# Row statistics of x taken once ahead of the scans, in a layer of a selective scan and a mixture of experts

## The chip, the cores and the metric

The program runs on one core of one Trainium2 chip. The metric is the device time of one execution in microseconds, and what is compared is the median over runs. Each core has five engines that work at the same time and wait for one another by semaphores: PE (TensorE, matmuls and transposes), DVE (VectorE), ACT (ScalarE), POOL (GpSimd) and SP (SyncE, which here only starts transfers). Transfers run on 16 DMA engines.

## What is computed

The input x has 4096 rows (tokens) of 256 numbers. Two sublayers follow one another, each of the form `x = x + layernorm(f(layernorm(x)))`. The first `f` is a selective scan, the second a router with the two best of 8 experts for each token plus a shared expert. Cut to what matters:

```python
xn = x * jax.lax.rsqrt(jnp.mean(x * x, -1, keepdims=True) + EPS) * norm_w   # x is layernorm(x) here
xg = xn @ in_proj_w
x_inner, gate = jnp.split(xg, 2, axis=-1)
x_inner = x_inner * jax.nn.silu(gate)
xc = causal_conv(x_inner, conv_w)                 # 4 taps, per channel
dt = jax.nn.softplus(xc @ dt_w + dt_b)
Bm, Cm = xc @ B_w, xc @ C_w
h = exp(dt * A) * h + dt * Bm * xc                # over time, for 512 channels x 16 states
y = sum_over_states(h * Cm) + D_skip * xc
out = y @ out_proj_w
...
x = x + _layernorm(selective_scan(_layernorm(x)))
x = x + _layernorm(experts(_layernorm(x)) + shared_expert(_layernorm(x)))
```

The layernorm of x and the rms norm after it need only the mean and the variance of each row of x, so the kernel takes both at once: one scale and one shift for each row.

## The kernel before

**Chunks and loops.** The 4096 rows are cut into 8 chunks of 512 (`NCH = 8`, `CH = 512`), a chunk into 4 row tiles of 128 rows (`J = 4`). A chunk is scanned in 64 slots (`SLOTS`, k = 0 to 63): one slot for each of 16 states times 4 groups of 128 channels. The outer loop runs from -2 to 9. In loop n the scans of chunk n stand slot by slot in each engine's program, and between them stands the work of other chunks: the projections of chunk n+1 (`*_proj`), the output, the norms and the routing of chunk n-1 (`*_post`), and the first norm of chunk n+2 (`*_lead`). In loops -2 and -1 there are no scans yet; this stretch is called the run-in here. After loop 9 the experts follow (71 row tiles).

**A slot.** ACT makes the decay `exp(dt*A)` (L735) into one of two banks. POOL multiplies the input (L1018) into one of four buffers. DVE scans over 512 steps (L861). PE turns the result of a state (L591), and DVE multiplies three quarters of it by C and adds it up (L878, L875), while ACT takes the fourth (L754). DVE runs on an input as soon as both the decay and the input are there.

**What sets the order.** Each engine runs its program strictly in the order in which it is written. Tables of slot numbers (`LEAD`, `PROJ` and `POST` for PE; `ACT_AT`, `DVE_AT`, `POOL_AT`) say behind which scan each piece of the other work stands. PE's results of this other work go in turn through three banks (`A`, `NQ = 3`); a bank is used again when its reader has emptied it (`room`). The list of turns comes from the same tables.

**The first norm of a chunk.** SP loads the chunk's x into `xp` (L348, slot 24). DVE takes `bn_stats` of 4 row tiles (L767, slot 48) and `bn_aggr` (L774, slot 49). POOL makes the variance term (L923, slot 50), ACT a first root by Ln and Exp (L615, L617, slot 51), POOL one Newton step of six small instructions (`newton`, L131 to L140, slot 53), then ACT normalizes the four tiles into `xn` (L624, slot 55), PE turns them (L439, slot 61) and ACT copies them into `xnT` (L628). For chunks 0 and 1 this stands in loops -2 and -1, for chunks 2 to 7 in loops 0 to 5, between scans.

**The run-in.** SP starts eight loads of weights and constants, then x of chunk 0, then the later weights (`late_weights`), then x of chunk 1. DVE scales `in_proj_w` by `norm_w` (L1153) and builds the four taps of the convolution as diagonal matrices (L1160), and all engines but SP wait for the end of this (`s_cst` at 5) before their loops. ACT first makes `-exp(A_log)` (L1105, L1107). Then chunk 0 passes through first norm, gates (PE L452), inner projection (PE L462, DVE L783), convolution (PE L472, ACT L647), B and C (`bT`: PE L480, ACT L652), dt (PE L491, ACT L663 to L670, POOL L939 and L943).

**Routing, at the end of a loop.** PE ranks the tokens of each expert (`rank`, L544 and L546, slot 60). DVE adds the result to the running base (`place`, L832, and `base`, L836) and multiplies the shared expert's three parts (`sgs`, L847), whose silu is done by ACT (L712, between two loads of its table).

Of the kernel before, what the change touches and what calls it, by code (L numbers as in the profile page):

```python
# [142 lines left out]
def program(nc, sem, sb, top, x_rows, out_rows, norm_w, in_proj_w, conv_w, dt_w, dt_b, A_log, B_w, C_w, D_skip,  # L143
# [619 lines left out]
    def dve_lead(e, k, c):  # L763
# [5 lines left out]
        if k == DVE_AT["stats_x"] + 1:  # L769
            e.wait_ge(s_cx, 2 * c + 1)  # L770
            if c:
                e.wait_ge(s_p0n, c)
# [722 lines left out]
```

## Time and profile before

| | us |
|---|---|
| median of 3 runs | 1716.26 |
| lowest and highest of them | 1711.7, 1716.83 |
| the profiled execution | 1713.8 |
| its span in the trace | 1712.0 |
| first scan starts | 80.49 |
| last scan starts | 1055.9 |

The profile is that of one execution. Its times count from the start of the span; the execution's own time is 1.8 us longer than the span. An engine counts as busy while an instruction of its runs. A matmul on 512 columns stands as two records in the trace.

### The profile page before, as it was taken

Reading aid. Unit: us, or ns where it says so; the run is one execution under the profiler, and the core shown is the slowest. Engines: PE = TensorE matmul, PEld = TensorE weight load, DVE = VectorE, ACT = ScalarE, POOL = GpSimd, SP = SyncE. Lnnn points to the kernel's source line nnn. Section 1 sums busy time; section 2 is a strip of 40 time slices with the busy share of each in tenths; the row PEclk is TensorE's granted clock in tenths of the full one; section 3 lists DMA queues with packets and bytes.
Section 4 is the critical chain, followed back from the end, with each engine's and each line's share of the span. In section 5 each row is a group of like instructions: output and inputs, shape, how many; then the busy total and the mean of one; then the engine's idle time right before and its main releaser. Section 6 shows DMA issues by size and latency. Waiting matters only on the chain.

```text
span 1712.0 us, 23925 instructions
## 1 busy us (share of the span) xinstructions
PE 1500.3 (88%) x6642; PEld 996.5 (58%) x6642; DVE 1353.0 (79%) x2425; ACT 1000.6 (58%) x1977; POOL 1043.6 (61%) x1233
## 2 busy tenths in 40 slices
PE   5888699899999998998998668699999999999990
PEld 2355455555655655745655555467677777777760
DVE  2199999899999899999899998256576676676665
ACT  3456667667668668659668564334454454454454
POOL 0478869979979879879889886312222322322224
PEclk9889899999999999999999968799999999999995
DMA  3011111311211221221211752523322222222216
GB/s 114 32 50 38 50 43 51 108 46 51 81 62 38 82 56 38 85 59 36 83 51 44 232 166 73 169 51 75 91 38 35 37 37 36 36 38 36 37 30 202
DMA packets 84398, 116.23 MB, mean 68 GB/s; under 512 B 11120, under 2 KB 58576, under 8 KB 84272
## 3 DMA queue, kind: packets, MB, share of 16 engines
q1 hardware_dynamic: 63344, 82.94, 16.0%
q0 software_dynamic: 16704, 27.57, 8.3%
q10 hardware_dynamic: 4224, 4.19, 0.7%
q8 instruction: 60, 0.98, 0.2%
q14 instruction: 66, 0.54, 0.1%
HBM read 81.05 MB, written 33.10 MB: 67 GB/s over the span
## 4 chain that ended last, share of the span: by engine, by line
PE 33%; POOL 6%; DVE 5%; issue 5%; ACT 2%; DMA 1%; SPq 0%; POOLq 0%; DVEq 0%; ACTq 0%
PE A L1244 10%; PE bA L1213 10%; PE bH L1213 10%; POOL arena L1018 4%; DVE arena L861 2%; DVE arena_t L878 1%; PE A L1235 1%; POOL expert_in_scratch L1006 1%; PE A L521 1%; DMA arena_t<-expert_in_scratch 0%; PE bH L591 0%; DMA sum_scratch<-arena_t 0%; DVE arena L878 0%; PE A L554 0%; DVE hT L1267 0%
## 5 line engine op out<-in xcount | busy, mean ns | idle before, releaser
L1018 POOL TENSOR_TENSOR arena<-arena 128x512 f32<-128x512 f32 x512 | 643.9, 1274 | 101.7 <-DVE arena L861 99.3
L735 ACT ACTIVATE bA<-arena,a_neg 128x512 f32<-128x512 f32 x512 | 352.1, 691 | 258.8 <-DVE arena L861 242.2
L591 PEld LDWEIGHTS bH<-ident,arena 128*128 128x128 f32 x2048 | 247.3, 146 | 303.0 <-DVE arena L861 139.3
L591 PE MATMUL bH<-ident,arena 128*128 128x128 f32 x2048 | 326.3, 287 | 93.9 <-DVE arena L861 72.9
L861 DVE TENSOR_TENSOR_SCAN arena<-bA,arena 128x512 f32<-128x512 f32 x256 | 305.7, 1210 | 63.6 <-ACT bA L735 48.8
L861 DVE TENSOR_TENSOR_SCAN arena<-bA,hl,arena 128x512 f32<-128x512 f32 x256 | 321.5, 1271 | 3.8 <-ACT bA L735 2.0
L1277 ACT COPY hT<-arena_t 32x160 f32<-32x160 f32 x568 | 182.5, 321 | 77.3 <-DVE arena_t L1261 71.6
L1267 DVE STREAM_TRANSPOSE hT<-arena_t 32x192 f32<-32x192 f32 x568 | 205.9, 363 | 6.6
L1371 POOL DMA_INDIRECT sum_scratch<-arena_t x71 | 113.5, 1598 | 148.6 <-issue 119.6
L1244 PE MATMUL A<-arena,hT 128*128 x852 | 197.5, 382 | 2.1 <-DVE hT L1267 2.1
L1365 POOL DMA_DIRECT2D arena_t<-expert_in_scratch x71 | 40.6, 573 | 257.5 <-issue 257.5
L1431 DVE TENSOR_TENSOR arena_t<-arena_t,bH 128x352 f32<-128x352 f32 x142 | 67.6, 518 | 151.1 <-PE bH L1213 151.1
L1213 PE MATMUL bA<-arena,arena_t 128*128 x568 | 181.5, 463 | 1.4 <-ACT arena_t L1413 1.4
L1213 PE MATMUL bH<-arena,arena_t 128*128 x568 | 179.6, 459 | 0.0
L1244 PEld LDWEIGHTS A<-arena,hT 128*128 128x128 f32 x852 | 157.6, 192 | 21.5 <-issue 2.5
L1213 PEld LDWEIGHTS bH<-arena,arena_t 128*128 128x128 f32 x568 | 107.9, 190 | 60.1
L1213 PEld LDWEIGHTS bA<-arena,arena_t 128*128 128x128 f32 x568 | 108.6, 192 | 51.3 <-issue 3.3
L878 DVE SCALAR_TENSOR_TENSOR arena<-bH,bc,arena 128x512 f32<-128x512 f32 x180 | 131.3, 729 | 5.7 <-PE bH L591 5.2
L878 DVE SCALAR_TENSOR_TENSOR arena_t<-bH,bc,arena_t 128x512 f32<-128x512 f32 x180 | 131.2, 729 | 3.8 <-PE bH L591 3.2
L472 PE MATMUL A<-arena 128*128 128x512 f32 x256 | 123.0, 593 | 0.0
L1413 ACT COPY arena_t<-A 128x256 f32<-128x256 f32 x71 | 26.5, 373 | 128.4 <-PE A L1235 128.4
L1407 ACT ACTIVATE arena_t<-bA 128x352 f32<-128x352 f32 x142 | 58.1, 461 | 72.6 <-PE bA L1213 72.6
(191 smaller groups left out, 2042.0 us busy)
## 6 DMA issues: line engine op xcount, KB each, us to landing
arena<-b_scratch SPq DMA_DIRECT2D x128, 256.0 KB, 3.2
arena_t<-expert_in_scratch POOLq DMA_DIRECT2D x71, 132.0 KB, 2.4
arena<-in_L_ffn_Wg_dram SPq DMA_DIRECT2D x8, 704.0 KB
arena<-in_L_ffn_Wu_dram SPq DMA_DIRECT2D x8, 704.0 KB
arena<-in_L_ffn_Wd_dram SPq DMA_DIRECT2D x8, 640.0 KB
arena<-in_L_attn_x_dram SPq DMA_DIRECT2D x8, 512.0 KB, 5.1
arena_x<-in_L_attn_x_dram SPq DMA_DIRECT2D x8, 512.0 KB, 5.1
x_scratch<-arena_x SPq DMA_DIRECT2D x8, 512.0 KB, 3.2
```

What stands on the lines that cost most here:

```text
L472: i = e.matmul(at(b, c)[:], w_tap[:, d, q, :], xin[:, d, q:q + CH], start=(q == 0), stop=(q == TAPS - 1))
L591: i = e.transpose(bH[g % NH][:, q * P:(q + 1) * P], hh[:, (n - 1) % 2, q, d * P:(d + 1) * P], ident[:])
L735: e.activation(bA[g % NA][:], dt[c % 2][:, d, :], ACT.Exp, scale=a_neg[:, d, n:n + 1]).then_inc(s_a, 1)
L861: e.tensor_tensor_scan(hh[:, n % 2, d, :], bA[g % NA][:], bb[:, k % NB, :], hl[:, n, d:d + 1] if c % 2 else 0.0, ALU.mult, ALU.add).then_i ...
L878: e.scalar_tensor_tensor(out=yy[:, d, :], in0=bH[g % NH][:], scalar=cm, in1=yy[:, d, :], op0=ALU.mult, op1=ALU.add).then_inc(s_y, 1)
L1018: e.tensor_tensor(bb[:, k % NB, :], u[c % 2][:, d, :], br[:, n % NR, :], ALU.mult).then_inc(s_bb, 1)
L1213: i = e.matmul(banks[f][:, 0:FH], xtT[:, t % 2, k, :], arena[:, bass.ds(ex * EW + (o + k * FI + f * FH), FH)], start=(k == 0), stop=(k == ...
L1244: i = e.matmul(bD[t % 2][:, 0:DM], hT[:, t % 2, q, :], arena[:, bass.ds(ex * EW + (2 * KD * FI + q * DM), DM)], start=(q == 0), stop=(q == ...
L1267: i = e.transpose(out, in_)
L1277: i = e.copy(out, in_)
L1371: e.indirect_dma_start(out=sh_d, out_offset=bass.IndirectOffsetOnAxis(ap=xt[:].bitcast(U32)[:, (t - 1) % NX, TOK:TOK + 1], axis=0), in_=yt ...
L1431: i = e.tensor_tensor(hm[:, t % 2, f * FH:(f + 1) * FH], sgm[:, t % 2, f * FH:(f + 1) * FH], bU[f][:, 0:FH], ALU.mult)
```

## The change

The mean and variance of x are no longer taken chunk by chunk between scans. They are taken in two groups: chunk 0 alone, first of all on DVE, and chunks 1 to 7 together (28 row tiles) in loop -1, behind the inner projection of chunk 0. For this SP loads x of chunks 1 to 7 a second time, 3.67 MB, into buffers that are still unused (`hh`, `bb`, `xf`), and `hs` holds the raw statistics. `mv`, `va`, `r0`, `tn` and `nmr` now hold all 32 row tiles. POOL's variance term and Newton step and ACT's two roots are done twice in all, in place of eight times. x of chunk 0 is the first transfer, ahead of the weights. The scaling of `in_proj_w` and the taps come behind the statistics of chunk 0 on DVE, `-exp(A_log)` behind the first norm on ACT, and the waits for `s_cst` are moved to where their data are used. The tables of slots are changed in some places.

```diff
-PROJ = {"gate0": 2, "gate1": 1, "gate2": 9, "gate3": 9, "inner0": 12, "inner1": 18, "inner2": 20, "inner3": 18, "cv0": 21, "cv1": 23, "cv2": 26,
-        "cv3": 30, "bT": 33, "dt0": 36, "bc": 37, "dt1": 42, "dt2": 45, "dt3": 50}
+PROJ = {"gate0": 2, "gate1": 1, "gate2": 9, "gate3": 8, "inner0": 12, "inner1": 17, "inner2": 20, "inner3": 18, "cv0": 21, "cv1": 23, "cv2": 26,
+        "cv3": 30, "bT": 33, "dt0": 36, "bc": 40, "dt1": 40, "dt2": 45, "dt3": 50}
...
-DVE_AT = {"stats_x": 48, "inner": (15, 19, 24, 21), "y": (9, 7, 5, 7), "stats_out": (19, 22), "stats_xf": 34, "logit": 52, "max": 54, "index": 54,
-          "place": 59, "base": 59, "position": 62, "sgs": (60, 63, SLOTS)}
+DVE_AT = {"inner": (15, 19, 24, 21), "y": (9, 7, 5, 7), "stats_out": (19, 22), "stats_xf": 35, "logit": 52, "max": 54, "index": 54, "place": 59,
+          "base": 60, "position": 63, "sgs": (SLOTS, 59, SLOTS + 1)}
...
+    STAGE = [(1, 4, row_tiles(hh[:].rearrange("p a b c -> p (a b c)"))), (5, 2, row_tiles(bb[:].rearrange("p a b -> p (a b)"))), (7, 1, xf[:, :, 0:DM])]
+    GROUP = [slice(0, J), slice(J, NCH * J)]
...
+    def sp_stage(e):
+        for c, n, to in STAGE:
+            e.dma_start(to, x_rows[c * CH:(c + n) * CH, :].rearrange("(r p) d -> p r d", p=P)).then_inc(s_xs, 16)
...
+    def dve_stats_x(e, g):
+        if g == 0:
+            e.wait_ge(s_x, 16)
+            tiles = [xp[:, j, :] for j in range(J)]
+        else:
+            e.wait_ge(s_xs, 16 * len(STAGE))
+            tiles = [to[:, j, :] for c, n, to in STAGE for j in range(n * J)]
+        for j, t in enumerate(tiles):
+            i = e.bn_stats(st[:, g * J + j, :], t)
+        i.then_inc(s_cx, 1)
+        e.wait_ge(s_cx, 2 * g + 1)
+        for j in range(len(tiles)):
+            i = e.bn_aggr(mv[:, g * J + j, :], st[:, g * J + j, :])
+        i.then_inc(s_cx, 1)
...
     def sync_scan(e):
+        e.dma_start(xp[:], rows_of(x_rows, 0)).then_inc(s_x, 16)
         e.dma_start(w_in[:], in_proj_w.rearrange("(k p) n -> p k n", p=P)).then_inc(s_w, 16)
...
             if loop == -1:
                 late_weights(e)
+                sp_stage(e)
...
+                if (loop, k) == (-1, 30):
+                    pool_var_x(e, 1)
+                if (loop, k) == (-1, 41):
+                    pool_norm_x(e, 1)
...
+                if (loop, k) == (-1, 38):
+                    act_root_x(e, 1)
...
+                if (loop, k) == (-1, 26):
+                    dve_stats_x(e, 1)
```

In the shared expert's work `su0` and `su1` change places (slots 58 and 62 become 62 and 58), `su2` goes from 62 to 63, ACT's copy of `bT` from 36 to 38, POOL's `halo` from 7 to 10.

Three places show how the instructions move. The first is the start of DVE's program; `arena` holds among others x, the weights and, in the new order, the staged rows; `ident` and `w_cv` make the taps. First the kernel before, then the changed one:

```order
1 L1149 MEMSET hT 64x2x128
2 L1153 TENSOR_SCALAR arena<-arena,w_nm 128x1024 x2
3 L1155 CAST iota_e<-iota_i 128x8
4 L1156 CAST base<-capi 128x8
5 L1160 TENSOR_SCALAR arena<-ident,w_cv 128x128 x16
6 L767 BN_STATS st<-arena 128x6 x4
7 L774 BN_AGGR mv<-st 128x2 x4
```

```order
1 L1178 MEMSET hT 64x2x128
2 L786 BN_STATS hs<-arena 128x6 x4
3 L790 BN_AGGR mv<-hs 128x2 x4
4 L1183 TENSOR_SCALAR arena<-arena,w_nm 128x1024 x2
5 L1185 CAST iota_e<-iota_i 128x8
6 L1186 CAST base<-capi 128x8
7 L1190 TENSOR_SCALAR arena<-ident,w_cv 128x128 x16
8 L799 TENSOR_TENSOR arena<-arena,A 128x512 x4
9 L786 BN_STATS hs<-arena 128x6 x24
10 L786 BN_STATS hs<-arena_x 128x6 x4
11 L790 BN_AGGR mv<-hs 128x2 x28
12 L877 SCALAR_TENSOR_TENSOR arena<-bA,arena 128x512 x6
```

The statistics of chunk 0 have moved ahead of the scaling and the taps, and all the others stand between the inner products (L799) and the first scans (L877, printed as SCALAR_TENSOR_TENSOR).

The second place is DVE at slots 59 to 61 of loop 1, behind the last scan that the ranks wait for; `pos` and `base` belong to the routing, `arena_x<-arena_x,A` is a part of `sgs`. Before, then changed:

```order
219 L832 TENSOR_TENSOR pos<-A,base 128x32
220 L836 TENSOR_TENSOR base<-base,A 128x8
221 L861 SCALAR_TENSOR_TENSOR arena<-bA,hl,arena 128x512
222 L847 TENSOR_TENSOR arena_x<-arena_x,A 128x512
223 L861 SCALAR_TENSOR_TENSOR arena<-bA,hl,arena 128x512
```

```order
215 L848 TENSOR_TENSOR pos<-A,base 128x32
216 L863 TENSOR_TENSOR arena_x<-arena_x,A 128x512
217 L877 SCALAR_TENSOR_TENSOR arena<-bA,hl,arena 128x512
218 L852 TENSOR_TENSOR base<-base,A 128x8
219 L877 SCALAR_TENSOR_TENSOR arena<-bA,hl,arena 128x512
```

One product of the shared expert now stands ahead of scan 60, and `base` behind it.

The third place is SP's queue behind the late weights, ahead of the first rows of B (`b_scratch`). Before, then changed:

```order
16 L428 DMA arena_x<-in_L_ffn_Sd_dram 96x256
17 L348 DMA arena<-in_L_attn_x_dram 128x4x256
18 L353 DMA b_scratch<-arena 16x512
19 L371 DMA arena<-b_scratch 128x512 x10
```

```order
16 L439 DMA arena_x<-in_L_ffn_Sd_dram 96x256
17 L359 DMA arena<-in_L_attn_x_dram 128x16x256
18 L359 DMA arena<-in_L_attn_x_dram 128x8x256
19 L359 DMA arena_x<-in_L_attn_x_dram 128x4x256
20 L355 DMA arena<-in_L_attn_x_dram 128x4x256
21 L364 DMA b_scratch<-arena 16x512
```

The three staging loads stand between the weights and the load of chunk 1's x.

## Rows read from the trace of the kernel before

**Rows 1.** The page's first line.

```profile
span 1712.0 us, 23925 instructions
```

**Rows 2.** Windows: length; busy us of PE, PEld, DVE, ACT, POOL; clock; DMA; GB/s.

```profile
197.00:320.00 123.00, 110.73 (x550) 68.40 (x549) 120.11 (x165) 87.49 (x143) 100.38 (x113) 1.00 0.19 58
320.00:441.00 121.00, 109.59 (x543) 68.88 (x542) 112.15 (x158) 86.12 (x140) 106.89 (x128) 1.00 0.20 58
```

**Rows 3.** Groups, DVE, 80 to 1057 us: busy us, mean ns | idle before.

```profile
L767 DVE BATCH_NORM_STATS2 st<-arena 128x6 f32<-128x256 f32 x24 | 8.3, 409 | 0.0
```

**Rows 4.** Timeline (start us, us) of DVE, slots 48 and 49 of loop 1.

```profile
286.88 1.39 DVE L767 BATCH_NORM_STATS2 st<-arena 128x6 f32<-128x256 f32 x4
288.18 1.28 DVE L861 TENSOR_TENSOR_SCAN arena<-bA,hl,arena 128x512 f32<-128x512 f32 x1
...
290.00 0.38 DVE L774 BATCH_NORM_AGGREGATE mv<-st 128x2 f32<-128x6 f32 x4
290.29 1.26 DVE L861 TENSOR_TENSOR_SCAN arena<-bA,hl,arena 128x512 f32<-128x512 f32 x1
```

**Rows 5.** Timeline of DVE, slots 59 to 61 of loop 1; [idle before <-releaser].

```profile
309.58 0.19 DVE L832 TENSOR_TENSOR pos<-A,base 128x32 f32<-128x32 f32 x1 [1.12 <-PE A L546]
309.81 0.16 DVE L836 TENSOR_TENSOR base<-base,A 128x8 f32<-128x8 f32 x1
310.55 1.28 DVE L861 TENSOR_TENSOR_SCAN arena<-bA,hl,arena 128x512 f32<-128x512 f32 x1 [0.57 <-ACT bA L735]
311.75 0.66 DVE L847 TENSOR_TENSOR arena_x<-arena_x,A 128x512 f32<-128x512 f32 x1
312.32 1.28 DVE L861 TENSOR_TENSOR_SCAN arena<-bA,hl,arena 128x512 f32<-128x512 f32 x1
```

**Rows 6.** ACT in order of time at the same place.

```profile
307.02 1.48 ACT L712 ACTIVATE arena_x<-arena_x 128x1536 f32<-128x1536 f32 x1
308.52 1.28 ACT L714 ACT_TABLE_LOAD   x1
309.82 1.30 ACT L735 ACTIVATE bA<-arena,a_neg 128x512 f32<-128x512 f32 x2
```

**Rows 7.** The run-in in order of time, all engines.

```profile
8.28 1.42 DVE L1153 TENSOR_SCALAR arena<-arena,w_nm 128x1024 f32<-128x1024 f32 x2 [6.96 <-DMA dskip<-in_L_attn_D_skip_dram]
...
13.01 1.41 DVE L767 BATCH_NORM_STATS2 st<-arena 128x6 f32<-128x256 f32 x4
...
22.25 9.92 PE L452 MATMUL A<-arena 128*128 128x512 f32 x16 [0.77 <-ACT arena L628]
...
40.04 0.69 DVE L783 TENSOR_TENSOR arena<-arena,A 128x512 f32<-128x512 f32 x1 [1.89 <-PE A L462]
...
57.29 0.57 ACT L652 COPY arena<-A 32x512 f32<-32x512 f32 x1 [3.89 <-PE A L480]
```

**Rows 8.** The end of the run-in in order of time.

```profile
73.75 0.63 ACT L670 ACTIVATE arena<-arena 128x512 f32<-128x512 f32 x1
...
75.14 2.07 ACT L624 ACTIVATE arena<-arena,nmr,r 128x256 f32<-128x256 f32 x4 [0.77 <-POOL nmr L140]
...
80.49 5.68 DVE L861 TENSOR_TENSOR_SCAN arena<-bA,arena 128x512 f32<-128x512 f32 x5 [38.03 <-ACT bA L735]
```

**Rows 9.** Line L348's loads of x; then windows, last column GB/s.

```profile
DMA to landing us min/median/max: 3.8/5.1/5.2
...
8.00:18.00 10.00, 0.00 (x0) 0.00 (x0) 6.48 (x28) 2.87 (x7) 1.42 (x8) 1.00 0.98 316
18.00:20.00 2.00, 0.45 (x2) 0.48 (x3) 0.00 (x0) 1.40 (x3) 0.00 (x0) 1.00 0.01 2
```

**Rows 10.** Groups, PE: gate matmuls of chunk 0 before and after 27.9 us.

```profile
L452 PE MATMUL A<-arena 128*128 128x512 f32 x7 | 6.1, 1043 | 0.8 <-ACT arena L628 0.8
...
L452 PE MATMUL A<-arena 128*128 128x512 f32 x9 | 4.2, 616 | 0.0
```

**Rows 11.** ACT's first norm during the scans, 100 to 1050 us.

```profile
L624 ACT ACTIVATE arena<-arena,nmr,r 128x256 f32<-128x256 f32 x24 | 12.5, 593 | 1.0 <-POOL nmr L140 1.0
```

More of the change, by code:

```diff
@@ L57 @@
-POOL_AT = {"var_x": 50, "norm_x": 53, "halo": 7, "skip": 36, "dt": (43, 49, 51, 58), "var_out": 23, "norm_out": 28, "add": (31, 31, 31, 31),
-           "var_xf": 38, "norm_xf": 40, "diff": 55, "token": 47, "chosen": 56, "picked": 61, "gates": SLOTS, "scatter": SLOTS + 1}
+        "su0": 62, "su1": 58, "su2": 63, "sd0": SLOTS + 3, "sd1": SLOTS + 7}
+ACT_AT = {"gate": (4, 3, 11, 10), "silu": 14, "conv": (26, 25, 28, 33), "bT": 38, "bc": 42, "dt": (40, 45, 49, 53), "norm_x": (55, 55, 55, 55),
+          "xnT": (60, 61), "out": (16, 19), "root_out": 27, "norm_out": (30, 31, 31, 31), "root_xf": 39, "xf": (41, 44, 44, 45), "xfT": (50, 46),
+          "e2": 60, "sg": (58, 56, 55), "sg_silu": 58, "sd": (SLOTS + 5, SLOTS + 8), "sum": 3}
@@ L60 @@
+DVE_AT = {"inner": (15, 19, 24, 21), "y": (9, 7, 5, 7), "stats_out": (19, 22), "stats_xf": 35, "logit": 52, "max": 54, "index": 54, "place": 59,
+          "base": 60, "position": 63, "sgs": (SLOTS, 59, SLOTS + 1)}
+POOL_AT = {"halo": 10, "skip": 36, "dt": (43, 49, 51, 58), "var_out": 23, "norm_out": 28, "add": (31, 31, 31, 31), "var_xf": 38, "norm_xf": 39,
+           "diff": 55, "token": 47, "chosen": 56, "picked": 61, "gates": SLOTS, "scatter": SLOTS + 1}
 LATE = {("sd0", NCH - 2): SLOTS + 24, ("sd1", NCH - 2): SLOTS + 26, ("sd", NCH - 2): (SLOTS + 26, SLOTS + 28),
@@ L759, in act_summed @@
             e.copy(xc[(c - 1) % 2][:, :, 0:P], bY[:].rearrange("p (d t) -> p d t", d=ND)).then_inc(s_y0, 1)
-    def dve_lead(e, k, c):
-        if k == DVE_AT["stats_x"]:
-            e.wait_ge(s_x, 16 * (c + 1))
-            for j in range(J):
-                i = e.bn_stats(st[:, j, :], xp[:, j, :])
-            i.then_inc(s_cx, 1)
[L769 to L772, printed above, removed]
-            for j in range(J):
-                i = e.bn_aggr(mv[:, j, :], st[:, j, :])
-            i.then_inc(s_cx, 1)
+    def dve_stats_x(e, g):
[12 more added lines that the diff above has]
+        i.then_inc(s_cx, 1)
     def dve_proj(e, k, c):
@@ L1130, in pe_scan @@
         e.wait_ge(s_id, 3)
-        e.wait_ge(s_cst, 5)
         for loop in range(-2, NCH + 2):
+            if loop == -1:
+                e.wait_ge(s_cst, 2)
             for k in range(SLOTS):
+                if (loop, k) == (-1, min(PROJ[name] for name in CONVS)):
+                    e.wait_ge(s_cst, 5)
                 if 0 <= loop < NCH or loop == NCH and k < ND:
```

78 lines of the change are left out of this document (39 added, 39 removed).

## The prediction

> **What bounds the kernel now.** I read the page first for the span, 1712.0 us [rows 1], and then cut it into stages: a run-in to the first scan at 80.49 us [rows 8], the scans, and the experts. The change touches the first two; the experts begin when the last chunk is routed and should only shift. So the question is what ends last in the run-in, and in a chunk of scans.
>
> For the scans I asked for busy time in stretches of one chunk. In an odd chunk DVE is busy 120.1 of 123 us, in an even one 112.2 of 121 [rows 2]. No other engine comes near in the odd one (PE 110.7, POOL 100.4, ACT 87.5); in the even one POOL follows with 106.9. DVE is thus the bound in odd chunks, with 2.9 us idle, and nearly so in even ones, with 8.9 us idle in which it waits in turn for ACT, POOL and PE. An instruction that leaves DVE's program between scans should give back its whole step, so long as the others can follow.
>
> For the run-in I read the instructions in order of time [rows 7, 8]. Chunk 0 goes through it as one chain: statistics at 13.01, gate matmuls at 22.25, inner product at 40.04, copy of `bT` at 57.29, last dt step of ACT at 73.75, first norm of chunk 1 at 75.14, first scan at 80.49. The statistics start at 13.01 without a wait [rows 7]: DVE had been working since 8.28 on the scaling and the taps, and had waited for the constants before that. DVE is idle from the inner products to the first scan, 38 us [rows 8].
>
> **The change, part by part.**
>
> *Run-in, start.* x of chunk 0 becomes the first transfer, issued where `in_proj_w` was, at about 0.9 us (an estimate: SP's first issue follows the start of all engines, the MEMSETs of which stand near 1 us). The loads of x took 3.8 to 5.2 us from issue to landing [rows 9]; the shortest is that of chunk 1, with nothing else under way. With 3.8 the statistics start at 4.7, with 5.2 at 6.1. I take 3.8, since nothing is ahead of it. From statistics to gate matmuls it took 22.25 - 13.01 = 9.24 us [rows 7], a chain over DVE, POOL, ACT and PE that is not changed. The gates then start at 14.0, which is 8.3 us earlier (6.9 with the late landing). They also need the scaled `in_proj_w`. Its data and all constants had landed by 8.28 [rows 7]; 0.5 MB more ahead of them costs 1.7 us at 316 GB/s [rows 9], so about 10.0, and the two scalings take 1.4: ready at 11.4, hidden by 2.6 us. The taps follow and end near 15, needed only by the convolution. ACT's `-exp(A_log)` moves into its wait for the gates. All of this shifts the chain by 8.3 us.
>
> Whether the whole chain shifts depends on the clock of PE. The gate matmuls up to 27.9 us took 1043 ns in the mean, those behind it 616 [rows 10]: first the lower of PE's two levels (1.2 GHz), then the upper (2.4). PE's first work stands just ahead of these. If the rise goes with that work, it moves too, and the gates keep their 8.3 us. If it came at a fixed time of the program, all gates up to 27.9 would be slow: 27.9 - 14.0 = 13.9 us at half speed in place of 27.9 - 22.25 = 5.65, a loss of (13.9 - 5.65)/2 = 4.1 us. The trace of before can't tell the two apart. The Trainium skill, page "TensorE: Matmul & The Clock Gate", Part 1, says that the default is the throttled clock and that activity of the array releases it; by that the first holds and the second, 4.1 us dearer, doesn't.
>
> *Run-in, end.* ACT finished dt at 74.38 (73.75 + 0.63) and waited 0.77 us for POOL's Newton step before it normalized chunk 1 [rows 8]. The step is now done long before, so 0.8 us more is gained, and the path stays norm, turn, copy, decay, scan. POOL's inputs, ready before ACT's first decay (the scan at 80.49 waited for ACT), come earlier by the same 8.3 us and by the Newton step that stood before them, so they don't hold the scan. The first scan starts at 80.5 - 8.3 - 0.8 = 71.4. **Term A: -9.1 us** (-7.7 with the late landing).
>
> *Staging.* 3.67 MB are added on SP's queue behind the late weights and ahead of chunk 1's x and of B's rows. The transfers up to then ended at 18 us, after 316 GB/s over ten microseconds, and the next two microseconds moved almost nothing [rows 9]; the bytes to that point are the same in the changed kernel. The staging ends at 18 + 3670/316 = 29.6 us. DVE comes to it behind the last inner product, at 40.04 + 0.69 - 8.3 = 32.4. Four `bn_stats` step DVE on by 288.18 - 286.88 = 1.30 us, four `bn_aggr` by 0.29 [rows 4]; 28 of each are 7 x 1.59 = 11.1 us, to 43.5. POOL's and ACT's small steps behind it are under 1.5 us. Queued behind the root on ACT is the copy of `bT`, due at 57.29 - 8.3 = 49.0 [rows 7], and behind that PE's next dt products, which need its bank. The slack is 49.0 - 1.5 - 43.5 = 4 us, and 2.8 us more for the transfer, which may land late without cost until DVE is there. The cover is DVE's idle stretch of 38 us; if it were gone the 11.1 us would be paid. Cost taken: nothing.
>
> *Scans.* `stats_x` leaves DVE in loops 0 to 5, for six chunks: 24 `bn_stats`, 8.3 us busy [rows 3], and 24 `bn_aggr`. Busy times overlap their neighbours; the step is 1.30 + 0.29 = 1.59 us [rows 4]. **Term B: 6 x 1.59 = -9.5 us.** With them go seven small instructions on POOL and two on ACT for each chunk. POOL is the nearest rival in even chunks, and what it loses is of the same size: its Newton steps take some 0.2 to 0.3 us each. So POOL doesn't keep DVE from the gain. ACT waited 1.0 us in all for the Newton step [rows 11]; I count half of it on the path. **Term C: -0.5 us.**
>
> *Slots 59 to 61.* There, once in each of loops 1 to 7, DVE waits 1.12 us for PE's ranks, does `place` and `base`, and waits 0.57 us for ACT's decay, which comes behind silu and a table load [rows 5, 6]. The changed order puts one `sgs` product into this second wait: it took a step of 312.32 - 311.75 = 0.57 us behind scan 60, and `base` (0.1 us of step) goes out of the wait. The first wait stays. Saved 0.57 - 0.1 = 0.47, seven times. **Term D: -3.3 us.** The product waits for ACT's silu, which ends at 308.5 [rows 6], and DVE gets there at 309.8 [rows 5]: 1.3 us of room. The other moved slots (gate3, inner1, dt1, bc, su2, halo) shift PE and POOL work by one to three slots, where PE has 10 us of idle time in a chunk; nothing for them, bounded by 0.3 us a chunk to either side, 2 us in all.
>
> *Discount.* ACT runs without a gap from silu to the decay of slot 60 [rows 6], so that DVE, 1.6 us ahead, may find it late in some chunks. Of term B I expect 1 us to be lost so.
>
> **Sum.** -9.1 - 9.5 - 0.5 - 3.3 + 1.0 = -21.4 us against the profiled execution's 1713.8 us, which gives 1692.4. The median of the runs shown is 2.5 us above it, 1716.3, and runs agree within 5 us; the same sum on the median gives **1695 us**. A change under 0.3%, 5 us, can't be told from none.
>
> **The rivals.**
>
> 1. *ACT and PE take back what DVE gives.* For: ACT has no gap ahead of slot 60 [rows 6], PE is busy 90% of a chunk [rows 2], and even chunks have waits for three engines. Against: both are only in places full, and ACT loses work too. If two thirds of B and all of C and D are lost: -9.1 - 3.2 = -12.3, **1704 us**.
> 2. *The clock rises at its own time.* The run-in gains 9.1 - 4.1 = 5.0 only: -17.3, **1699 us**. For it: nothing in the trace speaks against. The page's rule above is against it.
> 3. *The staging is late.* Chunk 1's x alone took 3.8 us for 0.5 MB [rows 9], 138 GB/s with its start. At that rate the staging takes 26.6 us, to 44.6, the statistics end at 55.7, and `bT` is copied at 57.2 in place of 49.0; PE has 1.7 us of other products first. Loss 6.5 us: -14.9, **1701 us**.
> 4. *Slower: the product at slot 59 holds DVE.* It needs ACT's silu and PE's `su1`. If ACT comes there later than DVE by d, each of 7 chunks pays d, and the end is slower when 7 d is over 21.4 us, d over 3.1 us. ACT would have to fall back by 1.3 + 3.1 = 4.4 us against DVE. At d = 4.1 it gives 1716.3 + 7 = **1723 us**. Against: ACT's work is less than before.
> 5. *Little changes*: both halves fail in part, within 5 us of **1716 us**.
>
> **How the numbers follow.** The forecast, 1691 to 1699 (landing at 5.2 us costs 1.4, the slots 2 to either side, the runs 2), has 0.68. Rival 1 has 0.14, rival 2 0.07, rival 3 0.05, rival 4 0.03, rival 5 0.03. All of the forecast and of 1 to 3 is over 0.3% faster: 0.94; within 0.3%: 0.03; slower: 0.03. The range takes in rivals 1 to 3 and 8 us below the forecast, for gains in waits that I have counted at nothing in the even chunks (8.9 us of DVE's idle time each): 1687 to 1706.
>
> **What would show it.** Term A: first scan at 71 to 73 us, gate matmuls at 14, the slow ones ending near 19.6. Staging: landed by 30, 28 `bn_stats` from 32.4, `bT` copied without a wait for POOL. Terms B to D: last scan 21 us earlier than 1055.9, so the scans 12 us shorter than 975, DVE's busy time 10 us less from first to last scan, its idle time in a chunk no longer than before; the wait for ACT at slot 60 gone, that for the ranks still 1.1 us. The prediction is wrong if DVE's idle time rises by more than 1 us in a chunk, if a wait for `s_sil` of the shared expert appears on DVE at slot 59, or if the experts' stage changes its length by more than 2 us.

## The result and the profile after

The changed kernel took 1688.57 us in the median of 4 runs (1687.43 to 1688.84), beside 1714.45 (1711.7 to 1716.83) for the kernel before: a ratio of 0.9848, interval 0.983 to 0.9867. The forecast was 1695, range 1687 to 1706. A second set on another chip gave 0.9859 (0.9844 to 0.9874). The profiled execution took 1688.78 us, 1.7 us longer than its span. The two spans differ by 24.9 us:

| stretch | before | after | difference |
|---|---|---|---|
| to the first scan | 80.5 | 70.7 | -9.8 |
| first to last scan | 975.4 | 961.5 | -13.9 |
| behind the last scan's start | 656.1 | 654.9 | -1.2 |

The page's first line and two windows, loops 1 and 2, with the columns of [rows 2]:

```profile
span 1687.1 us, 23869 instructions
...
181.50:303.10 121.60, 110.28 (x541) 68.06 (x540) 117.41 (x155) 86.77 (x140) 98.51 (x102) 0.99 0.20 59
303.10:426.60 123.50, 114.20 (x566) 71.61 (x565) 115.43 (x158) 87.70 (x142) 108.84 (x129) 1.00 0.19 61
```

They are cut at the scans that begin a loop, a little off the round cuts of [rows 2]. For the sum I took one window from first to last scan in each kernel, of before and of after:

```profile
80.50:1055.90 975.40, 860.31 (x4212) 547.97 (x4210) 928.22 (x1246) 666.87 (x1069) 830.82 (x941) 0.96 0.23 68
```

```profile
70.70:1032.20 961.50, 859.03 (x4211) 547.34 (x4210) 919.54 (x1196) 663.85 (x1057) 824.02 (x899) 0.96 0.22 69
```

DVE's busy time fell by 8.7 us, its idle time from 975.4 - 928.2 = 47.2 to 42.0, by 5.2. Only the first part is the statistics. This division, busy and idle time of DVE between first and last scan, is the measure used below.

**The run-in**, rows of all engines in order of time, to be read beside [rows 7, 8]:

```profile
4.96 1.41 DVE L786 BATCH_NORM_STATS2 hs<-arena 128x6 f32<-128x256 f32 x4 [3.65 <-DMA arena<-in_L_attn_x_dram]
...
9.81 1.42 DVE L1183 TENSOR_SCALAR arena<-arena,w_nm 128x1024 f32<-128x1024 f32 x2 [3.02 <-DMA dskip<-in_L_attn_D_skip_dram]
...
14.20 1.19 PE L463 MATMUL A<-arena 128*128 128x512 f32 x1 [0.77 <-ACT arena L643]
...
31.10 0.69 DVE L799 TENSOR_TENSOR arena<-arena,A 128x512 f32<-128x512 f32 x1 [1.86 <-PE A L473]
31.70 7.93 DVE L786 BATCH_NORM_STATS2 hs<-arena 128x6 f32<-128x256 f32 x24
39.55 1.39 DVE L786 BATCH_NORM_STATS2 hs<-arena_x 128x6 f32<-128x256 f32 x4
40.98 1.95 DVE L790 BATCH_NORM_AGGREGATE mv<-hs 128x2 f32<-128x6 f32 x28
...
44.36 0.23 ACT L626 ACTIVATE r<-va 128x28 f32<-128x28 f32 x1
...
48.35 0.57 ACT L667 COPY arena<-A 32x512 f32<-32x512 f32 x1 [3.50 <-PE A L491]
...
70.68 1.22 DVE L877 TENSOR_TENSOR_SCAN arena<-bA,arena 128x512 f32<-128x512 f32 x1 [27.75 <-ACT bA L750]
```

Every link stands within 0.8 us of where the sum put it: statistics 4.96 (4.7 forecast), `in_proj_w` scaled by 11.2 (11.4), gates 14.20 (14.0), group of 28 from 31.70 (32.4), `bT` copied at 48.35 (49.0), first scan 70.68 (71.4). The 28 `bn_stats` start without a wait, and the copy of `bT` waited for PE alone. The gate matmuls of chunk 0, in two windows that part at 18.9 us:

```profile
L463 PE MATMUL A<-arena 128*128 128x512 f32 x7 | 5.2, 905 | 0.8 <-ACT arena L643 0.8
...
L463 PE MATMUL A<-arena 128*128 128x512 f32 x11 | 4.9, 592 | 0.0
```

In the kernel before PE was slow until 27.9 us [rows 10]; now it is fast by 18.9. In the three kernels with the old run-in (the kernel before, and stats_only and new_tables of the experiments) the first gate matmul of under 600 ns starts at 26.7 to 28.2 us, in the eleven with the new one at 17.3 to 20.1. The rise of the clock went with PE's work and not with the time. That is what the Trainium skill says in "TensorE: Matmul & The Clock Gate", Part 1; by that page the gates keep their whole gain, and the trace agrees (14.20 to 22.25 is 8.05 us).

**In a loop.** DVE and ACT in loop 1, at the norm of the next chunk and at slots 59 to 61 [rows 4 to 6]:

```profile
288.53 1.28 DVE L877 TENSOR_TENSOR_SCAN arena<-bA,hl,arena 128x512 f32<-128x512 f32 x1 [0.56 <-ACT bA L750]
...
295.25 0.19 DVE L848 TENSOR_TENSOR pos<-A,base 128x32 f32<-128x32 f32 x1 [1.12 <-PE A L557]
295.35 0.68 DVE L863 TENSOR_TENSOR arena_x<-arena_x,A 128x512 f32<-128x512 f32 x1
296.21 1.28 DVE L877 TENSOR_TENSOR_SCAN arena<-bA,hl,arena 128x512 f32<-128x512 f32 x1 [0.18 <-ACT bA L750]
```

```profile
285.84 2.08 ACT L639 ACTIVATE arena<-arena,nmr,r 128x256 f32<-128x256 f32 x4
287.82 0.68 ACT L750 ACTIVATE bA<-arena,a_neg 128x512 f32<-128x512 f32 x1
...
295.49 1.30 ACT L750 ACTIVATE bA<-arena,a_neg 128x512 f32<-128x512 f32 x2
```

The product stands where the wait for ACT was, and 0.18 of 0.57 us is left; the wait for the ranks is still 1.12. New is a wait of 0.56 us at 288.53: DVE, no longer held by the statistics, comes to this scan while ACT is still in its four normalizations. In even loops the like happens with POOL. DVE in loop 4 before (the first two rows) and after:

```profile
659.20 1.22 DVE L861 TENSOR_TENSOR_SCAN arena<-bA,arena 128x512 f32<-128x512 f32 x1 [0.72 <-POOL hl L1030]
676.40 2.34 DVE L861 TENSOR_TENSOR_SCAN arena<-bA,arena 128x512 f32<-128x512 f32 x2 [1.40 <-ACT bA L735]
```

```profile
640.71 2.34 DVE L877 TENSOR_TENSOR_SCAN arena<-bA,arena 128x512 f32<-128x512 f32 x2 [0.32 <-POOL hl L1046]
648.53 1.22 DVE L877 TENSOR_TENSOR_SCAN arena<-bA,arena 128x512 f32<-128x512 f32 x1 [1.29 <-POOL hl L1046]
```

The wait of 1.40 us for ACT behind the normalizations is gone, and one of 1.29 for POOL's copy of the carried state (`hl`, made at every fourth slot) stands a few slots ahead of its place. POOL's five instructions ahead of that copy (642.08 to 648.19) follow one another without a gap, so the copy can't come earlier in this order. In loop 4 before, the time that DVE spent on statistics had covered this. The trace of before showed this already, in loop 6, which has no statistics and no norm of a next chunk:

```profile
916.67 1.22 DVE L861 TENSOR_TENSOR_SCAN arena<-bA,arena 128x512 f32<-128x512 f32 x1 [1.28 <-POOL hl L1030]
```

### The profile page after: what moved, and what is told of

It is laid out like the page before. It is cut to its first block, busy times and chain, and to the rows that moved or that the text cites. A ratio compares the mean times of both kernels' runs of the same rounds, so it can differ in the third digit from the quotient of the medians.

```text
span 1687.1 us, 23869 instructions
## 1 busy us (share of the span) xinstructions
PE 1494.5 (89%) x6642; PEld 993.3 (59%) x6642; DVE 1353.8 (80%) x2425; ACT 996.3 (59%) x1964; POOL 1038.9 (62%) x1191
## 4 chain that ended last, share of the span: by engine, by line
PE 33%; POOL 6%; DVE 5%; issue 5%; ACT 2%; DMA 2%; SPq 0%; POOLq 0%; DVEq 0%; ACTq 0%
PE A L1274 10%; PE bA L1243 10%; PE bH L1243 10%; POOL arena L1034 3%; DVE arena L877 2%; DVE arena_t L894 1%; PE A L1265 1%; DMA sum_scratch<-arena_t 1%; POOL expert_in_scratch L1022 1%; DMA arena_t<-expert_in_scratch 0%; PE bH L602 0%; PE A L532 0%; DVE arena L894 0%; ACT bA L750 0%; POOL rr L138 0%
## 5 line engine op out<-in xcount | busy, mean ns | idle before, releaser
L602 PEld LDWEIGHTS bH<-ident,arena 128*128 128x128 f32 x2048 | 250.9, 147 | 300.4 <-DVE arena L877 129.8
L877 DVE TENSOR_TENSOR_SCAN arena<-bA,arena 128x512 f32<-128x512 f32 x256 | 305.8, 1211 | 50.0 <-ACT bA L750 33.2
L877 DVE TENSOR_TENSOR_SCAN arena<-bA,hl,arena 128x512 f32<-128x512 f32 x256 | 321.6, 1271 | 2.5 <-ACT bA L750 2.1
L1274 PEld LDWEIGHTS A<-arena,hT 128*128 128x128 f32 x852 | 157.5, 191 | 21.4 <-issue 2.5
L769 ACT ACTIVATE hs<-bH,bc 128x512 f32<-128x512 f32 x128 | 87.5, 683 | 33.8 <-PE bH L602 32.5
```

The costliest lines, as they stand in the source:

```text
L602: i = e.transpose(bH[g % NH][:, q * P:(q + 1) * P], hh[:, (n - 1) % 2, q, d * P:(d + 1) * P], ident[:])
L769: e.activation(hs[:, q % 2, :], bH[(c * SLOTS + k) % NH][:], ACT.Identity, scale=bc[cs % 2][:, 0, NS + q % NS:NS + q % NS + 1]).then_inc(s ...
L877: e.tensor_tensor_scan(hh[:, n % 2, d, :], bA[g % NA][:], bb[:, k % NB, :], hl[:, n, d:d + 1] if c % 2 else 0.0, ALU.mult, ALU.add).then_i ...
L1274: i = e.matmul(bD[t % 2][:, 0:DM], hT[:, t % 2, q, :], arena[:, bass.ds(ex * EW + (2 * KD * FI + q * DM), DM)], start=(q == 0), stop=(q == ...
```

## The experiments

Four kernels ran on each of three chips, beside the kernel before, which took 1709.36, 1708.64 and 1709.6 us there. A saving against the kernel before is worked out from the ratio; from the medians it comes out up to 1 us different. Two kernels of one chip are compared by their medians. A ratio is known to some 0.0015, 2.5 us, so a difference of two ratios to some 0.002, 3.6 us. Two theories stand in the expectations. Theory 1: each part pays what the sum gave it. Theory 2: the total is made up otherwise, by the clock of PE in the first loop or by waits that other engines' work sets; its numbers were drawn anew after the first four runs, as the texts say.

| kernel | run-in | statistics once | new tables | ratio | interval | scans | busy DVE | idle DVE |
|---|---|---|---|---|---|---|---|---|
| before | | | | 1 | | 975.4 | 928.2 | 47.2 |
| runin_only | x | | | 0.9947 | 0.9933 to 0.9962 | 980.3 | 928.5 | 51.8 |
| stats_only | | x | | 0.9970 | 0.9961 to 0.9980 | 973.4 | 920.3 | 53.1 |
| new_tables | | | x | 0.9963 | 0.9948 to 0.9977 | 969.0 | 928.4 | 40.6 |
| old_tables | x | x | | 0.9919 | 0.9905 to 0.9934 | 970.6 | 920.1 | 50.5 |
| changed kernel | x | x | x | 0.9848 | 0.9830 to 0.9867 | 961.5 | 919.5 | 42.0 |

The last three columns are of one profiled execution each. That of runin_only took 1705.17 us where its median is 1700.78, so some 4 us of its idle time are not typical. The length of single loops in what follows is from these traces too, from first scan to first scan.

**runin_only**: the new order of the run-in and nothing else.

```diff
+        e.dma_start(xp[:], rows_of(x_rows, 0)).then_inc(s_x, 16)      # first of all on SP
...
+        dve_lead(e, DVE_AT["stats_x"], 0)                             # DVE, ahead of the scaling
+        dve_lead(e, DVE_AT["stats_x"] + 1, 0)
```

> The kernel before with the new order of the run-in alone: x of chunk 0 first, its statistics ahead of the scaling and the taps, the waits moved; the statistics of the other chunks stay between scans and the tables of slots are the old ones. Theory 1 (the sum of the prediction): 8.3 us less than the kernel before, first scan at 72.2 us, scans of unchanged length. Theory 2 (what the changed kernel's trace suggests: the first loop of scans also gains, because the granted clock of PE was back at 1.00 at 83 us there and only near 120 us before): about 10.5 us less, the first loop of scans some 2.3 us shorter than 116.0.

It took 1700.78 us beside 1709.36, 9 us less, with the first scan at 72.4. The run-in pays its term and the first loop keeps its length (116.1 us, before 116.0). Theory 2's guess that a better clock in loop 0 comes with the earlier start has no support here: over the first 35 us of scans the granted clock is 0.77, before 0.78.

**stats_only**: statistics once, but x of chunk 0 loaded and taken in the old order, and the old tables; the diff is against the changed kernel.

```diff
-        e.dma_start(xp[:], rows_of(x_rows, 0)).then_inc(s_x, 16)
         e.dma_start(w_in[:], in_proj_w.rearrange("(k p) n -> p k n", p=P)).then_inc(s_w, 16)
...
+        e.dma_start(xp[:], rows_of(x_rows, 0)).then_inc(s_x, 16)
```

> The changed kernel with the old order of the run-in (x of chunk 0 behind the weights, its statistics behind the taps) and the old tables of slots: the statistics of chunks 1 to 7 in one group are what is left of the change. Theory 1: 9.5 + 0.5 + 0.8 = 10.8 us less than the kernel before, 1.6 us in each of loops 0 to 5. Theory 2 (odd loops give DVE's time back as waits for ACT and PE, even loops gain on POOL): about 8 to 9 us less, with at most 1 us in loops 1, 3 and 5 and 2 us or more in loops 0, 2 and 4.

1703.98 us, 5.1 less than before; both theories expected more (10.8, and 8 to 9). The first scan is 1.4 us earlier (79.04), and from first to last scan DVE is busy 7.9 us less and idle 5.9 us more. Most of the step that DVE saves is taken back by waits. Against the kernel before, loops 0, 2 and 4 are 1.9, 0.3 and 2.4 us shorter, loops 1 and 3 are 1.5 and 0.5 longer and loop 5 is 0.4 shorter. So the pattern is roughly that of Theory 2, and the sizes are smaller.

**old_tables**: the changed kernel with the old tables. One of their lines:

```diff
-DVE_AT = {"inner": (15, 19, 24, 21), ... "place": 59, "base": 60, "position": 63, "sgs": (SLOTS, 59, SLOTS + 1)}
+DVE_AT = {"inner": (15, 19, 24, 21), ... "place": 59, "base": 59, "position": 62, "sgs": (60, 63, SLOTS)}
```

> The changed kernel with the old tables of slots. Theory 1: 3.3 us slower than the changed kernel, DVE waits 0.5 us for ACT at slot 60 again. Theory 2 (the tables gave at slot 60 and took it back as waits for PE near slot 14 of odd loops, 1.3 us in loop 1): within 1.5 us of the changed kernel.

1695.55 us, 0.9919: the sum of the two savings before it, 14 us. It is slower than the changed kernel by 0.0060 to 0.0071, 10 to 12 us, so both theories failed (3.3, and within 1.5). Where the statistics' step goes in an odd loop is seen in loop 3, DVE's rows that have a wait, and then PE at the end of the loop:

```profile
539.00 1.28 DVE L877 TENSOR_TENSOR_SCAN arena<-bA,hl,arena 128x512 f32<-128x512 f32 x1 [0.56 <-ACT bA L750]
...
545.71 0.19 DVE L848 TENSOR_TENSOR pos<-A,base 128x32 f32<-128x32 f32 x1 [1.12 <-PE A L557]
...
546.61 1.28 DVE L877 TENSOR_TENSOR_SCAN arena<-bA,hl,arena 128x512 f32<-128x512 f32 x1 [0.51 <-ACT bA L750]
...
553.94 0.75 DVE L894 SCALAR_TENSOR_TENSOR arena_t<-bH,bc,arena_t 128x512 f32<-128x512 f32 x1 [0.42 <-PE bH L602]
554.87 0.69 DVE L863 TENSOR_TENSOR arena_x<-arena_x,A 128x512 f32<-128x512 f32 x1 [0.18 <-PE A L574]
```

```profile
546.00 0.60 PE L450 MATMUL A<-ident,arena 128*128 128x128 f32 x4
548.62 1.09 PE L450 MATMUL A<-ident,arena 128*128 128x128 f32 x4 [2.01 <-DVE arena_x L863]
...
551.20 2.26 PE L574 MATMUL A<-arena_x 128*128 128x512 f32 x4
553.30 0.60 PE L602 MATMUL bH<-ident,arena 128*128 128x128 f32 x4
```

```profile
546.00:556.00 10.00, 7.99 (x35) 5.43 (x34) 8.89 (x13) 5.51 (x10) 7.26 (x11) 0.83 0.27 82
```

Of 1.59 us, 0.56 go to ACT's normalizations, 0.6 to PE, whose turn of a state stands behind four records of the shared expert's products (L574), and 0.21 to another wait for PE. The 0.6 us go with PE's clock. PE waited 2.01 us for a bank that DVE's product `sgs` empties; behind that wait the same four matmuls take 1.09 us in place of 0.60, and the granted clock of the stretch is 0.83 (last row). In loop 5 of stats_only the clock stays at 1.00 there, and the 0.6 us are missing.

This wait of PE, 1.9 to 2.2 us, stands in each of loops 1 to 5 of all six kernels with the old tables, the kernel before among them, and in none of the eight with the new ones, where this product stands at slot 59 and not at 60. Beside 15 of these 30 waits the granted clock fell, and in those loops DVE then waited 0.2 to 2.2 us for PE at the loop's end; beside the other 15 it didn't. In loops 1 to 5 of the eight kernels with the new tables the clock fell at a loop's end once in 40. So a part of what the tables give, 2.5 us of DVE's idle time in old_tables and 0.7 in the kernel before, is a clock that stays up, as far as these traces show it; no run isolates it.

Loops 1, 3 and 5 took 123.5, 123.7 and 124.0 us, where the kernel before took 122.1, 123.3 and 123.5. The even loops 2 and 4 took 125.3 and 123.8, before 125.6 and 126.2.

**new_tables**: the kernel before with the new slots for the work that stays.

```diff
-DVE_AT = {"stats_x": 48, ... "place": 59, "base": 59, "position": 62, "sgs": (60, 63, SLOTS)}
+DVE_AT = {"stats_x": 48, ... "place": 59, "base": 60, "position": 63, "sgs": (SLOTS, 59, SLOTS + 1)}
```

> The kernel before with the new tables of slots alone; statistics and run-in as before. Theory 1: 3.3 us less than the kernel before. Theory 2: within 1.5 us of it, with DVE's wait for PE longer near slot 14 of odd loops.

1703.32 us, 6.3 less (3.9 to 8.9), with DVE's busy time unchanged and 6.6 us less of idle time: about twice term D, and far from Theory 2's 1.5. The waits for ACT at slot 60 fell from 3.3 us over loops 1 to 7 to 1.3, less than forecast. The rest came from elsewhere: 1.6 us of it lie in loop 0, most of them in waits for PE, and at the end of loop 4 the wait for PE at the low clock (0.7 us) is gone. At the start of loops 2, 4 and 6 DVE waited for POOL's `hl` 2.97, 2.75 and 2.78 us before and 2.37, 2.17 and 2.17 here, later in them 0.7 and now 0.3 us, and in the odd loops three waits of 0.6 us for POOL's input are gone, while PE's turn is waited for 0.35 us longer there (0.9 in loop 1). One row of it, DVE in loop 2:

```profile
334.98 2.34 DVE L861 TENSOR_TENSOR_SCAN arena<-bA,arena 128x512 f32<-128x512 f32 x2 [2.37 <-POOL hl L1030]
```

With the new table two products `sgs` (0.6 us each) stand behind the first scan of a loop, in place of one. DVE does the second one where it would wait for POOL anyway. The sizes fit, but that this entry alone does it was argued and not tried.

**after_again, early_hl, spread_norm, both**: the changed kernel once more, and two edits to it and their union.

> The changed kernel once more, beside which the next three stand. Theory 1 (each part pays what the sum gave it) and Theory 2 (the run-in pays its 9 us, the statistics half of their step, the new tables twice or more of theirs) both expect what was measured: 1686 to 1690 us, 1.3 to 1.7% under the kernel before.

0.9859 (0.9844 to 0.9874), 1684.55 us beside 1708.64.

```diff
-        if c % 2 == 0 and k % ND == ND - 1 and k > ND:      # pool_last, the copy of hl
+        if c % 2 == 0 and k % ND == 0 and k >= ND:          # three slots earlier
```

> The changed kernel with POOL's copy of the carried state moved by one step: at the first of four products of a pair of scans in place of the last of the four. In the changed kernel DVE waits for that copy 2.5 to 5.0 us in each even loop, 17 us in all. If these waits have taken the place of what the removed statistics gave (Theory 2), most of them go away: 8 to 14 us faster than the changed kernel, 1675 to 1680, with no POOL wait above 0.3 us in a loop. If POOL's throughput is the bound there (rival), the copy only pushes POOL's next products later, the waits for POOL come back at another instruction, and the time stays within 3 us of the changed kernel.

1677.27 us, 0.9818 (0.9804 to 0.9831): 7.3 us faster than the changed kernel, just under the 8 to 14 expected and well over the rival's 3, and DVE idle 34.0 us. POOL and DVE at the start of loop 2, first in the changed kernel:

```profile
316.20 1.00 POOL L1022 DMA_INDIRECT expert_in_scratch<-arena_x,posl  x1 [0.17 <-issue]
317.50 0.97 POOL L1022 DMA_INDIRECT expert_in_scratch<-arena_x,posl  x1 [0.30 <-issue]
318.50 2.50 POOL L1034 TENSOR_TENSOR arena<-arena 128x512 f32<-128x512 f32 x2
320.94 0.18 POOL L1046 COPY hl<-arena 128x4 f32<-128x4 f32 x1
321.25 2.34 DVE L877 TENSOR_TENSOR_SCAN arena<-bA,arena 128x512 f32<-128x512 f32 x2 [2.39 <-POOL hl L1046]
```

```profile
318.58 2.45 DVE L877 TENSOR_TENSOR_SCAN arena<-bA,arena 128x512 f32<-128x512 f32 x2
...
324.77 1.22 DVE L877 TENSOR_TENSOR_SCAN arena<-bA,arena 128x512 f32<-128x512 f32 x1 [0.80 <-POOL arena L1034]
```

The copy stood behind POOL's scattering of rows for the experts. Moved ahead of it, all waits for `hl` are gone from loops 2, 4 and 6 (5.0 us in loop 2), and about 3 us of it stay gained in each; 0.8 us come back at the next input of POOL and 1.3 us as waits for PE. In loop 0, 2.6 us of waits for `hl` are gone too, but the loop is no shorter (110.9 us beside 110.8 and 110.1). So POOL was partly late by order and partly by amount, between the theory and its rival.

```diff
-  ... "norm_x": (55, 55, 55, 55), ...
+  ... "norm_x": (54, 55, 56, 57), ...
```

> The changed kernel with ACT's four normalizations of the next chunk at slots 54, 55, 56 and 57, in place of four behind each other at slot 55. They are a burst of about 2 us, in which ACT's decays stand behind them. If the burst is what makes DVE wait for ACT (0.56 us in each odd loop, about 1 us in each even one), the waits at that place vanish and it is 2 to 5 us faster than the changed kernel. The rival: the normalization feeds the transposes and the gates of the next chunk, and spreading it makes DVE's wait for PE longer by as much; then it is within 2 us.

1692.15 us, 0.9899 (0.9884 to 0.9914): slower than the changed kernel by 7.6 us. Both expectations failed (2 to 5 us faster, and within 2). ACT and DVE in loop 3:

```profile
537.30 0.59 ACT L639 ACTIVATE arena<-arena,nmr,r 128x256 f32<-128x256 f32 x1
...
539.00 1.28 ACT L727 ACT_TABLE_LOAD   x1
...
543.09 1.30 ACT L750 ACTIVATE bA<-arena,a_neg 128x512 f32<-128x512 f32 x2
```

```profile
537.40 1.28 DVE L877 TENSOR_TENSOR_SCAN arena<-bA,hl,arena 128x512 f32<-128x512 f32 x1 [0.51 <-ACT bA L750]
...
543.82 1.28 DVE L877 TENSOR_TENSOR_SCAN arena<-bA,hl,arena 128x512 f32<-128x512 f32 x1 [0.75 <-ACT bA L750]
```

From the normalizations to the decay of slot 60 ACT has next to no gap, so the wait for the burst stays as 0.51 us, one slot on, and with less room before silu the wait at slot 60, gone from this loop in the changed kernel, is back with 0.75. In each of loops 1 to 5 the idle time is 0.6 to 0.9 us longer than in after_again. Spreading the burst moved its wait and added one.

> The changed kernel with both edits, the earlier copy of the carried state and the spread normalization. If the two kinds of wait are independent, the gains add: 10 to 17 us faster than the changed kernel, 1671 to 1677. If one engine behind both is full, the second edit adds nothing to the better of the two.

1681.0 us, 0.9841 (0.9828 to 0.9855). It is 3.6 us faster than the changed kernel, not 10 to 17, and the other expectation, that the second edit adds nothing, failed too: it costs 3.7 us on top of the first. early_hl is the best kernel of this study.

**runin_early and old_early**: runin_only and old_tables, each with the early copy.

> The kernel before with the new order of the run-in and POOL's copy of the carried state three slots earlier; per-chunk statistics and old tables stay. It is the base of old_early. In the kernel before DVE waited for the copy only a few us in all, so Theory 2 expects little more than the run-in alone gave: 1695 to 1701 us, 0 to 5 us under runin_only as it stood to its kernel before (0.9947). If POOL was a hidden limit all along, it is 8 us or more.

1692.86 us (1687.62 to 1694.37), 0.9898 (0.9883 to 0.9913). It is 0.0049, 8 us, under runin_only, and lies below the range of 1695 to 1701. The text on record says that the kernel before waited "only a few us in all" for the copy. That was a misreading: it waited 4.4, 4.1 and 5.4 us in loops 2, 4 and 6. POOL's copy was a limit before the change too, and Theory 2 had this wrong.

> The same with the statistics of all chunks ahead of the scans, still with the old tables. Against runin_early this is the worth of the removed statistics (1.59 us of DVE's step in each of six loops, 9.5 us) once POOL's copy does not stand in the way. Without the early copy it was about 5 us on the medians, with the even loops gaining and the odd ones nothing. Theory 2 (waits for POOL take back the gain in even loops, waits for ACT and PE that in odd loops) expects loops 2 and 4 shorter by 2.5 us or more than in runin_early and loops 1, 3 and 5 within 0.7 us of it: 6 to 9 us faster in all. The rival, that DVE's program as a whole is no longer the bound, expects no loop to be shorter by more than 1 us, and under 4 us in all. If the full step is paid in every loop, it is 9.5 us or more.

1686.39 us (1683.05 to 1689.15), 0.9859 (0.9844 to 0.9874): 6.5 us under runin_early, in the band of Theory 2, but the two ratios leave 3 to 10 us, so neither the rival (under 4) nor the full step (9.5) is quite out. The other half of Theory 2 isn't borne out: loops 2 and 4 took 122.6 and 122.5 us, in runin_early 122.7 and 122.4. The two profiled executions took 1687.69 and 1689.15 us, the one near the lowest of its runs and the other the highest. A part of this is seen: in loops 2, 4 and 5 of old_early the clock fell beside PE's wait for `sgs`, and DVE waited 0.7, 0.8 and 1.9 us for PE behind it, in runin_early nothing in these loops. Even without that, loops 2 and 4 would be only some 0.8 us shorter. How the 6.5 us fall on the loops stays open.

**late2 and late4**: 2.1 and 4.2 MB more of x loaded ahead of the staging, awaited by the statistics.

```diff
+    EXTRA = [dt[1], u[1]]                    # late4: and xc[1], yT[1]
...
+        for i, to in enumerate(EXTRA):
+            e.dma_start(row_tiles(to.rearrange("p a b -> p (a b)")), x_rows[0:2 * CH, :].rearrange("(r p) d -> p r d", p=P)).then_inc(s_xs, 16)
```

> The changed kernel with 2.1 MB more loaded ahead of the staging, awaited by the statistics. At some 350 GB/s that is 6 us: the staging lands near 34 to 36 us, in place of 29, the 28 bn_stats run from there to 46 or 47, and ACT's root is at 48, where the copy of bT (48.4) is due. By the prediction's slack (4 us and 2.8 us) it costs nothing: within 1.5 us of the changed kernel, first scan 71 to 72.5. If the cover is thinner than that, the first scan comes later by up to 4 us.

> The same with 4.2 MB more, 12 us of transfer: landed at 40 to 42, statistics to 52 or 53, ACT's root behind 54, the copy of bT there in place of 48.4, 5.5 to 6.5 us late, of which PE has up to 1.7 us of other products: first scan at 74 to 77 and the kernel 3.5 to 6.5 us slower than the changed one. If the cover is DVE's whole idle stretch to the first scan (the rival: ACT's queue doesn't matter), it costs nothing.

late2 took 1686.22 us, 0.9864 (0.9849 to 0.9879), first scan 70.2: no cost, though its statistics began at 35.37, 3.7 us late. late4 took 1689.93 us, 0.9886 (0.9871 to 0.9901), first scan 72.9. Rows of late4, DVE and ACT:

```profile
41.43 7.94 DVE L789 BATCH_NORM_STATS2 hs<-arena 128x6 f32<-128x256 f32 x24 [9.29 <-DMA arena_x<-in_L_attn_x_dram]
...
53.00 0.23 ACT L629 ACTIVATE r<-va 128x28 f32<-128x28 f32 x1 [8.18 <-POOL va L940]
...
53.39 0.56 ACT L670 COPY arena<-A 32x512 f32<-32x512 f32 x1
```

The statistics begin 9.7 us late, the copy of `bT` comes 5.0 us late, and the first scan 2.2 us late (1.5 beside after_again). ACT's queue is thus what makes lateness cost: ACT sat 8.18 us in the root's wait with the copy of `bT` behind it. The room is real: statistics 3.7 us late cost nothing, 9.7 us late cost about 2 us of the first scan, where 74 to 77 was expected: of the 5.0 us at `bT` the chain of dt takes 2.8 back. The median is 3.7 us over that of late2, at the low end of the 3.5 to 6.5 expected, but as uncertain as that, and only about 2 of it are seen in the trace; the scans aren't longer (959.7 us).

## Why the prediction was right

The time came out 6.4 us below the likeliest value, below the 1691 to 1699 that had 0.68, and inside the range only by the 4 us below 1691 that were left for gains not counted. 1.8 us of the 6.4 come from the kernel before, whose median is now 1714.45 and was 1716.26 in the sum. The saving itself is 26 us where 21.4 was forecast. By its steps:

- **Term A** (-9.1): right, in size and link by link. runin_only measured -9.1 +- 2.5 us, the trace of the changed kernel -9.8.
- **Staging** (nothing): right. The transfers ran at 344 GB/s from 18 to 28 us and 318 in the next 2 (316 was taken), and were done by 30. late2 and late4 put the edge of the cover between statistics 3.7 and 9.7 us late; the prediction had 4.
- **Term B with the discount and term C** (-9.5 + 1.0 - 0.5 = -9.0): near in the total of the changed kernel, and there by luck in part. Against new_tables, which lacks only this and the run-in, DVE is busy 8.9 us less and idle 1.3 us more in the scans, so -7.5. But 3.1 us of that lie in loop 0, where the step is 1.59, and loops 1 to 5 gave only 0.8 to 1.2 us each, half to three quarters of the step. "Should give back its whole step" is not what happened in a chunk. With the old tables it is only about -5 us (stats_only -5.1, of which 1.4 in the run-in; old_tables under runin_only by 0.0028, -4.8), because there the idle time is 3 to 6 us longer than before. Term C isn't seen by itself.
- **Term D** (-3.3): the step that was mis-sized. The place is right and gives 2 us of the 3.3 (waits at slot 60 of 3.3 us in all before, 1.3 in new_tables, 1.7 in the changed kernel). But "the other moved slots: nothing, 2 us in all" failed: the tables give 6.3 us alone, and 0.0060 to 0.0071, 10 to 12 us, on top of the rest, since they also open the places (ACT at slot 60, PE at a loop's end with its clock) that take back term B. The even loops' 8.9 us of idle time that were counted at nothing were waits with a price, about half of them for POOL's `hl`: 4.4, 4.1 and 5.4 us in loops 2, 4 and 6.
- **Rival 1** (ACT and PE take back what DVE gives) happened with the old tables for most of the step, and in loops 1 to 5 for a quarter to a half of it with the new ones. **Rival 2** is refuted by the gates at 14.20 and their fast part, which begins by 18.9 (its price was put a little high: by [rows 10] a slow gate matmul took 1.7 times a fast one and not twice, which makes 3.4 us of the 4.1), **rival 3** by the landing before 30 us. **Rival 4**, the product that waits for silu: no wait of it at 295.35. **Rival 5** is out by the time.

Of the signs announced, two were missed in size: DVE's idle time rose by 1.3 us in loop 1 of this profile (0.4 in after_again), over the 1 us that was to refute the sum, and the scans came 13.9 us shorter in place of 12. The total of the scans is near the forecast by two errors that cancel: the first loop became 5.2 us shorter (116.0 to 110.8) where 1.6 was forecast, and loops 1 to 7 together 8.6 where the sum has some 11. Open is how the 4 to 5 us that the whole is better than the three parts alone (0.53 + 0.30 + 0.37 = 1.2% beside 1.41 to 1.52%) are divided; the ratios' own uncertainty is nearly as large. PE's clock in the first loop was low, with breaks, until 113 us before and until 76 us after:

```profile
80.00:100.00 20.00, 17.95 (x63) 9.95 (x64) 17.39 (x18) 12.15 (x20) 17.57 (x18) 0.77 0.12 41
100.00:120.00 20.00, 15.75 (x65) 9.77 (x65) 18.33 (x22) 13.62 (x17) 12.96 (x13) 0.83 0.24 58
```

```profile
80.00:100.00 20.00, 13.99 (x76) 8.79 (x75) 18.80 (x22) 15.44 (x20) 14.84 (x17) 1.00 0.13 44
```

The first two rows are of before, the last of after. The clock is not the main cause of the short first loop. late2, late4 and after_again have the changed kernel's program in this loop, and over the first 35 us of scans the granted clock was 0.83, 0.90 and 0.96 (before 0.78, after 0.92), while the loop took 111.9, 110.1 and 110.1 us. So 0.83 in place of 0.96 goes with 1.8 us in these traces, of the 5.2. Of single parts the tables give 2.1 us in this loop (113.9), the statistics 1.9 (114.1), the run-in nothing (116.1), and run-in and statistics together 4.3 (old_tables, 111.7); why these two do more together is open.

## What to carry to other kernels

Split DVE's (or the bound engine's) time into busy and idle between two fixed events: removing work shows in the first, planning in the second. Here the first fell by 8.7 us and the second by 5.2, although the removed work alone made it grow. Before an instruction is taken out, look for a stretch of the same trace that already lacks it: loop 6 of the kernel before had the 1.28 us wait that took the freed time in loop 4. A small instruction on which the bound engine waits belongs ahead of the long ones on its engine: one copy of 0.18 us moved by three slots gave 7 us, as much as the tables planned anew gave alone (6). And where a product of the bound engine frees a bank that PE waits for, its place can bear on PE's clock too.

## What was not expected of the hardware

- The staging moved at 344 GB/s from 18 to 28 us, above the 316 GB/s of the loads before it [rows 9], and 4.2 MB more (late4) kept that rate to the end.
- POOL's start of one indirect transfer held it for 0.97 to 1.25 us, with 0.17 to 0.30 us of issue ahead (316.20, 317.50): the eight at the start of loop 2 of the changed kernel come in pairs of 2.5 to 2.8 us, 10 us in all in which no product is made.
- PE's granted clock fell beside waits of PE of only 1.9 to 2.2 us, in 15 of 30 cases (2.01 us at 548.62 in old_tables, where the next four matmuls took 1.09 us in place of 0.60).
